# Layer 1 of a two-layer attention kernel: q loaded in the preceding slot, four coefficient instructions, GpSimd's last low part behind the next row's first combination

## Chip, core and metric

One core of one Trainium2 chip runs the whole program. The metric is the device time of one execution in microseconds. The median of the runs shown is compared, and one further execution was profiled.

## What is computed

Two layers, each added to its input. Layer 0 is a four-headed attention behind a convolution; the change does not touch it. Layer 1, for each of B = 2 images of C = 192 channels and N = 64 x 64 = 4096 positions, with xf the normalised image as [N, C]:

```python
xn = (xf - mu) * jax.lax.rsqrt(var + EPS) * ln_w + ln_b
Q, K, V = xn @ Wq.T, xn @ Wk.T, xn @ Wv.T
S = jnp.einsum('bnd,bmd->bnm', Q, K)
attn1 = jax.nn.softmax(S, axis=-1)
attn2 = jnp.square(jax.nn.relu(S))
e1, e2 = (jnp.exp(w1), jnp.exp(w2))
attn = e1 / (e1 + e2) * attn1 + e2 / (e1 + e2) * attn2
out = jnp.einsum('bnm,bmd->bnd', attn, V)      # then back to [b, c, h, w], + x
```

## The kernel before

Layer 1 takes an image after the other. A prologue makes, for the image, the scores' operand `kst` and the values `v_hl` in SBUF and the queries in `q_scratch` in HBM, all split into two float16 parts. Then the row loop runs over RB = 32 rows of 128 queries. A row's 4096 scores are worked in NQ = 4 pieces of 1024 columns. Each engine has its own hand-written sequence, cut into slots; in slot t VectorE and ScalarE finish row t and begin row t + 1, while TensorE makes the scores of row t + 1 and multiplies row t - 1's weights by v. Four slots stand alone, then a hardware loop holds two slots a pass (its branch lies between an odd slot and the next even one), and the last two stand alone. Semaphores alone tie the engines.

For piece c of a row, in order:

- TensorE, `score_half` (L1338): ten matmuls into PSUM `ps_s`, two groups of five. One group and one group of eight weighing matmuls (`weigh_group`, L1351) alternate, eight pairs a slot; `turn_output` (L1361) transposes the output of row t - 2 before the third weighing group.
- VectorE, `maximum` (L1578): `neg` = scaled, negated scores, with the piece's minimum as an accumulated output. `maximum` 3 is followed by L1583, L1585 (`m1`, one element per partition) and L1587 (`inv`), and frees PSUM for TensorE.
- ScalarE: `relu` and `square` (L1176, L1181) into `sqr[s]`, which is `vb` or `rn`; `exp_piece` (L1187) into `prob[s]`, which lies in `gp`, with the sums; `factors` (L1193) four factors of the row.
- VectorE, `coefficients` (L1593 to L1603): six small instructions, of [128, 1] or [128, 4], from sums and factors to `coef`.
- VectorE, `combine` (L1610), here called combination c: prob = prob x coef + sqr, 1024 columns, both tensors in SBUF.
- High part: `p_hi` = prob in float16; GpSimd casts pieces 0 and 1 (L1125), ScalarE pieces 2 and 3 (`high`, L1201). Low part: `p_lo` = prob - p_hi, all four on GpSimd (L1129), in the order high 0, low 0, high 1, low 1, low 2, low 3. Low 2 waits for combination 3 of its row.
- SyncE's queue: `turn_chunk` sends each part through a transposing DMA (L1066 high, L1068 low) into `at_hi`, `at_lo`, which TensorE weighs with v. Behind piece 0 stand `load_q` of row t + 2 (L1047), `store` of row t - 2 (L1058) and `load_res` (L1053).

VectorE's slot t: combination 3 of row t - 1; `copy_output` of row t - 2 (L1615, L1618: PSUM to `ob`, scaled by `back`); maximum 0 of row t + 1; coefficients of row t; combination 0; maximum 1; combination 1; `add_output` of row t - 2 (L1628, from PSUM and `res`); maximum 2; combination 2; maximum 3.

Of the kernel before, what the change touches and what calls it, by code (L numbers as in the profile page):

```python
# [817 lines left out]
def layer1(nc, x, o_dram, weights, consts, m_dram, r_dram, res_dram, q_dram, out):  # L818
# [6 lines left out]
    with ExitStack() as ctx:  # L825
# [16 lines left out]
        MX, CO = NQ + 3, 6  # L842
        KC = KT // NQ
        HIGH_ACT = (2, 3)
# [109 lines left out]
        relued = sem("relued")  # L954
        exped = sem("exped1")
        squared = sem("squared")
        c_op = sem("c_op")
        p_made = sem("p_made")
        t_full = sem("t_full")
        hi_made = [sem(f"hi_made{i}") for i in range(NQ)]  # L960
        lo_made = sem("lo_made1")
# [14 lines left out]
        with nc.Block() as block:  # L976
            @block.sync
            def _(sp):
# [8 lines left out]
                def image(b):  # L987
# [73 lines left out]
                    def turn_chunk(row, s, c, first=False):  # L1061
# [5 lines left out]
                        sp.wait_ge(lo_made, NQ * (RB * b + row) + c + 1)  # L1067
# [15 lines left out]
                    load_q(1, 1)  # L1083
                    slot(0, 0, True)
                    slot(1, 1, True)
                    for t in range(2, RB):
                        slot(t, t % 2, more_q=t < RB - 2)
# [9 lines left out]
            def _(pool):  # L1097
# [6 lines left out]
                for b in range(B):  # L1104
# [13 lines left out]
                    def split(row, s, first=False):  # L1118
                        for c in range(NQ):
                            cols = slice(c * QB, (c + 1) * QB)  # L1120
                            if c not in HIGH_ACT:
                                pool.wait_ge(p_made, NQ * (RB * b + row) + c + 1)
                                if not first:
                                    pool.wait_ge(turned[c], 32 * (RB * b + row))
                                pool.tensor_copy(p_hi[:, cols], prob[s][:, cols]).then_inc(hi_made[c], 1)  # L1125
                            pool.wait_ge(hi_made[c], RB * b + row + 1)
                            if c == 2:
                                pool.wait_ge(p_made, NQ * (RB * b + row) + NQ)
                            pool.tensor_tensor(p_lo[:, cols], prob[s][:, cols], p_hi[:, cols], ALU.subtract).then_inc(lo_made, 1)  # L1129

                    for row in range(RB):
                        split(row, row % 2, row == 0 and b == 0)

            @block.scalar
            def _(act):
# [3 lines left out]
                for b in range(B):  # L1139
# [31 lines left out]
                    def relu(row, s, c, first=False):  # L1171
                        cols = slice(c * QB, (c + 1) * QB)
                        act.wait_ge(mx_op, MX * (RB * b + row) + c + 1)
                        if not first:
                            act.wait_ge(p_made, NQ * (RB * b + row - 2) + c + 1)
                        act.activation(sqr[s][:, cols], neg[:, c, :], ACT.Relu, scale=top[:, 3:4]).then_inc(relued, 1)  # L1176

                    def square(row, s, c):
                        cols = slice(c * QB, (c + 1) * QB)
                        act.wait_ge(relued, NQ * (RB * b + row) + c + 1)  # L1180
                        act.activation(sqr[s][:, cols], sqr[s][:, cols], ACT.Square, scale=inv[:, s:s + 1]).then_inc(squared, 1)  # L1181

                    def exp_piece(row, s, c, first=False):
                        act.wait_ge(mx_op, MX * (RB * b + row) + c + 1)
                        if not first:
                            act.wait_ge(lo_made, NQ * (RB * b + row - 2) + c + 1)
                        act.activation(prob[s][:, c * QB:(c + 1) * QB], neg[:, c, :], ACT.Exp,  # L1187
                                       bias=nbias[:, s, c:c + 1], scale=-1.0,
                                       accum_out=sums[:, s, c:c + 1]).then_inc(exped, 1)

                    def factors(row, s):
# [559 lines left out]
```

## Time and profile before

| | us |
|---|---|
| median of 3 runs | 3659.16 (3658.95 to 3661.98) |
| the profiled execution's own time | 3657.04 |
| its span in the trace | 3655.3 |
| PE busy over the span | 3214.4 (88%) |
| DVE busy | 2191.9 (60%) |
| ACT busy | 2117.3 (58%) |
| POOL busy | 1023.0 (28%) |

The first image's row loop fills about 2257 to 2869 us, the second's about 3043 to 3653; the rest is layer 0 and the images' prologues. PE is TensorE, DVE VectorE, ACT ScalarE, POOL GpSimd, SPq the queue of SyncE. A row in order of time has its start in us from the span's start, its duration in us, engine, line, operation, output <- inputs, shape, and how many instructions in a row of the same kind were merged; in brackets stand the idle time of the engine before it and what ended it. An instruction of VectorE that stands in line behind another shows a start some 0.08 us ahead of the other's end. "issue" means that the engine waited for nothing that the profile shows. A row on stretches of time has the stretch, its length, then busy time (and number of instructions) of PE, PEld, DVE, ACT and POOL, the granted TensorE clock as a share of full speed, the share of the DMA engines and GB/s. A row on one line of code has the number of instructions and the shortest, median and longest duration in ns.

### The profile page before, as it was taken

How to read it: one execution, taken by the hardware profiler on the slowest of the kernel's cores; microseconds unless marked ns; L12 is line 12 of the kernel's file. 1: busy time of each engine (PE TensorE's matmuls, PEld its weight loads, DVE VectorE, ACT ScalarE, POOL GpSimd, SP SyncE). 2: the span in 40 equal slices, each digit the busy share in tenths (PEclk: the TensorE clock that was granted, in tenths of full speed). 3: DMA queues.
4: the chain of work that ended last, by engine and by line, in shares of the span. 5: the costliest groups of instructions: out<-in, count | busy, mean ns of one | idle time of the engine just before them, and what ended most of it. 6: DMA issues, size and time to landing. Idle time of an engine off the chain costs nothing. (4 is left out here: it accounts for less than half of the span.)

```text
span 3655.3 us, 48153 instructions
## 1 busy us (share of the span) xinstructions
PE 3214.4 (88%) x16424; PEld 1273.0 (35%) x16424; DVE 2191.9 (60%) x2585; ACT 2117.3 (58%) x2306; POOL 1023.0 (28%) x510
## 2 busy tenths in 40 slices
PE   1249999999999999999999768999999668999998
PEld 0012222222322223222222224555555334555554
DVE  4755254552446523475210255999999547999997
ACT  0016655556555565555666314888888126888886
POOL 0211002111021020110200032555555233555555
PEclk9669999999999999999999879999999789999999
DMA  6130213112121121220200223766666534766666
GB/s 183 44 75 19 59 40 70 43 33 59 41 62 42 41 58 42 45 56 24 57 10 7 67 77 94 133 131 132 130 130 130 120 100 101 133 130 133 129 130 124
DMA packets 691174, 295.70 MB, mean 81 GB/s; under 512 B 603314, under 2 KB 645042, under 8 KB 689266
## 3 DMA queue, kind: packets, MB, share of 16 engines
q1 hardware_dynamic: 690996, 293.45, 37.4%
q8 instruction: 96, 1.57, 0.2%
q14 instruction: 82, 0.67, 0.1%
HBM read 95.46 MB, written 34.28 MB: 35 GB/s over the span
## 5 line engine op out<-in xcount | busy, mean ns | idle before, releaser
L440 ACT ACTIVATE prob<-ps_s,cur 128x1024 f32<-128x1024 f32 x1024 | 1084.5, 1110 | 738.5 <-PE ps_s L514 737.0
L527 PE MATMUL ps_a<-prob,vt 128*64 128x512 f32 x4096 | 995.2, 607 | 0.0
L1338 PE MATMUL ps_s<-kst,qs 128*128 128x512 f16 x2560 | 638.5, 382 | 67.7 <-DMA qs<-q_scratch 65.3
L1129 POOL TENSOR_TENSOR p_lo<-gp,p_hi 128x1024 f16<-128x1024 f32 x256 | 547.4, 2139 | 321.2 <-DVE gp L1610 281.1
L1351 PE MATMUL ps_o<-v_hl,at_hi 128*128 128x384 f16 x2048 | 553.4, 331 | 22.6 <-DMA at_lo<-p_lo 19.7
L508 PE MATMUL ps_s<-q_a,k_a 128*128 128x512 f16 x2048 | 534.6, 383 | 7.3 <-issue 2.9
L1351 PE MATMUL ps_o<-v_hl,at_lo 128*128 128x192 f16 x2048 | 507.9, 249 | 0.0
L527 PEld LDWEIGHTS ps_a<-prob,vt 128*64 128x64 f32 x4096 | 249.1, 136 | 411.8 <-issue 410.2
L1338 PEld LDWEIGHTS ps_s<-kst,qs 128*128 128x128 f16 x2560 | 240.3, 98 | 306.8 <-issue 79.8
L1578 DVE TENSOR_SCALAR_CACHE_REDUCE neg<-ps_s,mix 128x1024 f32<-128x1024 f32 x256 | 326.1, 1274 | 23.6 <-PE ps_s L1338 23.4
L508 PEld LDWEIGHTS ps_s<-q_a,k_a 128*128 128x128 f16 x2048 | 137.9, 97 | 516.2 <-ACT prob L440 436.9
L411 POOL TENSOR_TENSOR sq<-qk 112x1024 f32<-112x1024 f32 x32 | 59.6, 1892 | 919.3 <-DVE qk L610 919.3
L610 DVE SCALAR_TENSOR_TENSOR qk<-pad,vec,qk 112x2048 f32<-112x2048 f32 x128 | 290.3, 2345 | 0.0
L1187 ACT ACTIVATE gp<-neg,nbias 128x1024 f32<-128x1024 f32 x256 | 290.2, 1133 | 0.0
L685 DVE RECIPROCAL rden<-rden 128x512 f32<-128x512 f32 x32 | 107.3, 3353 | 296.6 <-DMA rden<-den_scratch 296.6
L1351 PEld LDWEIGHTS ps_o<-v_hl,at_hi 128*128 128x128 f16 x2048 | 202.7, 99 | 203.6 <-DMA at_lo<-p_lo 45.4
L1610 DVE SCALAR_TENSOR_TENSOR gp<-gp,coef,rn 128x1024 f32<-128x1024 f32 x128 | 259.2, 2028 | 17.9 <-DVE neg L1578 7.9
L1610 DVE SCALAR_TENSOR_TENSOR gp<-gp,coef,vb 128x1024 f32<-128x1024 f32 x128 | 259.9, 2030 | 11.5 <-DVE neg L1578 4.7
L593 DVE TENSOR_SCALAR pad<-ps_h,vec 112x512 f32<-112x512 f32 x96 | 72.2, 752 | 291.5 <-PE ps_h L457 291.3
L457 PE MATMUL ps_h<-z,w 96*112 96x512 f32 x384 | 187.8, 624 | 38.8 <-DMA z<-z_scratch 38.8
L1351 PEld LDWEIGHTS ps_o<-v_hl,at_lo 128*128 128x128 f16 x2048 | 202.8, 99 | 44.3 <-issue 0.5
L1176 ACT ACTIVATE vb<-neg,top 128x1024 f32<-128x1024 f32 x128 | 146.0, 1141 | 116.5 <-DVE neg L1578 116.2
(176 smaller groups left out, 2865.1 us busy)
## 6 DMA issues: line engine op xcount, KB each, us to landing
z<-z_scratch SPq DMA_DIRECT2D x96, 384.0 KB, 3.8
sq<-rn_scratch SPq DMA_DIRECT2D x16, 768.0 KB, 10.4
qs<-q_scratch SPq DMA_DIRECT2D x64, 128.0 KB, 2.5
gn_x<-in_x SPq DMA_DIRECT2D x4, 1536.0 KB, 18.6
z_scratch<-gn_x SPq DMA_DIRECT2D x4, 1536.0 KB, 11.6
q_a<-hi SPq DMA_DIRECT2D x64, 96.0 KB, 2.3
rden<-den_scratch SPq DMA_DIRECT2D x64, 96.0 KB, 2.2
o_scratch<-o_s SPq DMA_DIRECT2D x64, 96.0 KB, 1.9
```

Of the source, the lines that this page charges most:

```text
L440: act.activation(prob[:, a % PR, :], ps_s[:, a % 2, :], ACT.Exp, bias=cur[:, slot:slot + 1], scale=1.0 / SPLIT).then_inc(exped, 1)
L457: ins = pe.matmul(ps_h[0:KR, bank, :], w[:, slot, t, 0:KR], z[:, c % ZS, t, :], start=(t == 0), stop=(t == CT - 1))
L508: pe.matmul(ps_s[:, n % 2, h * CH:(h + 1) * CH], k_a[:, slot, m * P:(m + 1) * P], q_a[:, slot, cols], start=True, stop=False)
L527: ins = pe.matmul(ps_a[h * HALF:(h + 1) * HALF, j % 2, :], vt[:, slot, m, :], prob[:, a % PR, h * CH:(h + 1) * CH], start=(m == 0), stop=( ...
L610: ins = dve.scalar_tensor_tensor(out=out, in0=src, scalar=vec[0:KR, slot, 1 + tap:2 + tap], in1=out, op0=ALU.mult, op1=ALU.add)
L1129: pool.tensor_tensor(p_lo[:, cols], prob[s][:, cols], p_hi[:, cols], ALU.subtract).then_inc(lo_made, 1)
L1176: act.activation(sqr[s][:, cols], neg[:, c, :], ACT.Relu, scale=top[:, 3:4]).then_inc(relued, 1)
L1187: act.activation(prob[s][:, c * QB:(c + 1) * QB], neg[:, c, :], ACT.Exp, bias=nbias[:, s, c:c + 1], scale=-1.0, accum_out=sums[:, s, c:c + ...
L1338: ins = pe.matmul(ps_s[:, c % 2, h * CH:(h + 1) * CH], qs[:, s, qt, :], kst[:, ktile, cols], start=(t == 0), stop=(t == len(terms) - 1))
L1351: ins = pe.matmul(ps_o[:, s * CH:s * CH + wide], a[:, s, kt, :], v_hl[:, kt, 0:wide], start=(kt == 0 and t == 0), stop=(kt == KT - 1 and t ...
L1578: dve.tensor_scalar(neg[:, c, :], ps_s[:, c % 2, :], mix[:, 6:7], None, ALU.mult, ALU.min, accum_out=nbias[:, s, c:c + 1]).then_inc(mx_op, 1)
L1610: dve.scalar_tensor_tensor(out=prob[s][:, cols], in0=prob[s][:, cols], scalar=coef[:, s, c:c + 1], in1=sqr[s][:, cols], op0=ALU.mult, op1= ...
```

## The change

- `load_q(t + 3)` stands in slot t before the transpositions of piece 3, into the buffer that row t + 1 leaves; rows 0 to 2 are loaded ahead. Before, `load_q(t + 2)` stood behind those of piece 0.
- `coefficients` has four instructions: `back` first, with `mix[:, 5:6]` in the place of a constant; then product, scaling by `back` and sum in one, with an accumulated output; reciprocal; `coef`. It gets a wait for `ob_made`, an earlier instruction of VectorE itself. `relu` no longer carries the scale, which moves into L1585's counterpart (L1615), now a constant factor and a minimum against `top[:, 3:4]`; `top[:, 3:4]` is made once, with one more small instruction.
- GpSimd's low 2 no longer waits for combination 3; low 3 waits for combination 0 of the next row.
- VectorE's `add_output` stands behind combination 2, before maximum 3.
- ScalarE's slot begins with square 0, which was third; it waits for `inv`.
- Semaphores per piece (`p_made[c]`, `exped[c]` and others) take the place of shared counters, and rows outside the image are skipped in the functions (`live`) instead of by flags. The order of the first and last slots is as it was but for the moves above.

```diff
@@ sync
                         for c in range(NQ):
+                            if c == NQ - 1 and more_q:
+                                load_q(t + 3, 1 - s)
                             turn_chunk(t, s, c, first and t < 2 and b == 0)
                             if c == 0:
-                                if more_q:
-                                    load_q(t + 2, s)
                                 if not first:
                                     store(t - 2, s)
@@ gpsimd
+                    def low(row, s, c):
+                        if not 0 <= row < RB:
+                            return
+                        cols = slice(c * QB, (c + 1) * QB)
+                        pool.wait_ge(hi_made[c], RB * b + row + 1)
+                        if c == 3 and row < RB - 1:
+                            pool.wait_ge(p_made[0], RB * b + row + 2)
+                        pool.tensor_tensor(p_lo[:, cols], prob[s][:, cols], p_hi[:, cols], ALU.subtract).then_inc(lo_made[c], 1)
+
+                    def slot(t, s):
+                        high(t, s, 0)
+                        low(t, s, 0)
+                        high(t, s, 1)
+                        low(t, s, 1)
+                        low(t, s, 2)
+                        low(t, s, 3)
@@ scalar
-                        exp_piece(t, s, NQ - 1, older)
+                        square(t, s, 0)
+                        exp_piece(t, s, 3)
                         factors(t, s)
-                        square(t, s, 0)
@@ vector
-                            dve.tensor_scalar(m1[:, s:s + 1], nbmin[:, s:s + 1], mix[:, 7:8], -1.0, ALU.mult, ALU.min).then_inc(mx_op, 1)
+                            dve.tensor_scalar(m1[:, s:s + 1], nbmin[:, s:s + 1], 1.0 / GAIN, top[:, 3:4], ALU.mult, ALU.min).then_inc(mx_op, 1)
                     def coefficients(row, s):
...
-                        dve.tensor_tensor(part[:, :], fac[:, s, :], sums[:, s, :], ALU.mult).then_inc(c_op, 1)
+                        if not isinstance(row, int) or row > 1:
+                            dve.wait_ge(ob_made, RB * b + row - 1)
+                        dve.scalar_tensor_tensor(out=back[:, s:s + 1], in0=m1[:, s:s + 1], scalar=mix[:, 5:6],
+                                                 in1=m1[:, s:s + 1], op0=ALU.mult, op1=ALU.mult).then_inc(c_op, 1)
                         dve.wait_ge(c_op, at + 1)
-                        dve.tensor_reduce(total[:, :], part[:, :], AX_X, ALU.add).then_inc(c_op, 1)
-                        dve.scalar_tensor_tensor(out=back[:, s:s + 1], in0=m1[:, s:s + 1], scalar=1.0 / (GAIN * GAIN),
-                                                 in1=m1[:, s:s + 1], op0=ALU.mult, op1=ALU.mult).then_inc(c_op, 1)
+                        dve.scalar_tensor_tensor(out=part[:, :], in0=fac[:, s, :], scalar=back[:, s:s + 1], in1=sums[:, s, :],
+                                                 op0=ALU.mult, op1=ALU.mult, accum_out=total[:, :]).then_inc(c_op, 1)
+                        dve.wait_ge(c_op, at + 2)
+                        dve.reciprocal(total[:, :], total[:, :]).then_inc(c_op, 1)
                         dve.wait_ge(c_op, at + 3)
-                        dve.tensor_tensor(total[:, :], total[:, :], back[:, s:s + 1], ALU.mult).then_inc(c_op, 1)
+                        dve.tensor_scalar(coef[:, s, :], fac[:, s, :], total[:, 0:1], mix[:, 4:5], ALU.mult, ALU.mult).then_inc(c_op, 1)
...
+                        maximum(t + 1, 1 - s, 2)
                         combine(t, s, 2)
-                        if new:
-                            maximum(t + 1, 1 - s, 3)
+                        add_output(t - 2, s, j)
+                        maximum(t + 1, 1 - s, 3)
```

GpSimd, one slot late in an image, before (with the semaphores each instruction waits for; `hi_made3` stands at low 3):

```order
384 L1125 CAST p_hi<-gp 128x1024 [waits turned0,p_made]
385 L1129 TENSOR_TENSOR p_lo<-gp,p_hi 128x1024 [waits hi_made0]
386 L1125 CAST p_hi<-gp 128x1024 [waits turned1,p_made]
387 L1129 TENSOR_TENSOR p_lo<-gp,p_hi 128x1024 [waits hi_made1]
388 L1129 TENSOR_TENSOR p_lo<-gp,p_hi 128x1024 [waits p_made,hi_made2]
389 L1129 TENSOR_TENSOR p_lo<-gp,p_hi 128x1024 [waits hi_made3]
```

The same place after the change (`p_made1_0` is combination 0):

```order
384 L1125 CAST p_hi<-gp 128x1024 [waits turned0,p_made1_0]
385 L1134 TENSOR_TENSOR p_lo<-gp,p_hi 128x1024 [waits hi_made0]
386 L1125 CAST p_hi<-gp 128x1024 [waits turned1,p_made1_1]
387 L1134 TENSOR_TENSOR p_lo<-gp,p_hi 128x1024 [waits hi_made1]
388 L1134 TENSOR_TENSOR p_lo<-gp,p_hi 128x1024 [waits hi_made2]
389 L1134 TENSOR_TENSOR p_lo<-gp,p_hi 128x1024 [waits p_made1_0,hi_made3]
```

The instructions stand in the same order; the wait for a combination moved from low 2 to low 3, and there it is the next row's.

VectorE in the loop, from combination 1 to maximum 3's end, before:

```order
1049 L1610 SCALAR_TENSOR_TENSOR gp<-gp,coef,rn 128x1024 [waits mx_op,squared]
1050 L1628 SCALAR_TENSOR_TENSOR ot<-ps_t,unscale,res 96x128 [waits ot_out1,res_in1,t_full]
1051 L1628 SCALAR_TENSOR_TENSOR ot<-ps_t,unscale,res 96x128
1052 L1575 REGISTER_ALU
1053 L1577 REGISTER_ALU [waits s_full]
1054 L1578 TENSOR_SCALAR neg,nbias<-ps_s,mix 128x1024 [waits exped1]
1055 L1580 REGISTER_ALU
1056 L1610 SCALAR_TENSOR_TENSOR gp<-gp,coef,rn 128x1024 [waits mx_op,squared]
```

After the change:

```order
1011 L1644 SCALAR_TENSOR_TENSOR gp<-gp,coef,rn 128x1024 [waits mx_op,squared1_1]
1012 L1605 REGISTER_ALU
1013 L1608 TENSOR_SCALAR neg,nbias<-ps_s,mix 128x1024 [waits exped1_2,s_full]
1014 L1610 REGISTER_ALU
1015 L1644 SCALAR_TENSOR_TENSOR gp<-gp,coef,rn 128x1024 [waits mx_op,squared1_2]
1016 L1666 SCALAR_TENSOR_TENSOR ot<-ps_t,unscale,res 96x128 [waits ot_out1,res_in1,t_full]
1017 L1666 SCALAR_TENSOR_TENSOR ot<-ps_t,unscale,res 96x128
```

The two instructions of `add_output` moved from before maximum 2 to behind combination 2.

## Rows read from the trace of the kernel before

**Rows 1.** Busy time by stretch, the first image's row loop.
```profile
2301.00:2836.00 535.00, 496.64 (x3061) 279.55 (x3059) 505.26 (x719) 435.53 (x547) 307.11 (x174) 1.00 0.68 131
```

**Rows 2.** Order of time, DVE, one slot of the loop, combination 0 to coefficients.
```profile
2453.40 0.29 DVE L1603 TENSOR_SCALAR coef<-fac,total,mix 128x4 f32<-128x4 f32 x1
2453.73 1.28 DVE L1610 SCALAR_TENSOR_TENSOR gp<-gp,coef,vb 128x1024 f32<-128x1024 f32 x1
...
2456.37 3.04 DVE L1610 SCALAR_TENSOR_TENSOR gp<-gp,coef,vb 128x1024 f32<-128x1024 f32 x1 [0.15 <-DVE neg L1578]
2459.33 0.59 DVE L1628 SCALAR_TENSOR_TENSOR ot<-ps_t,unscale,res 96x128 f32<-96x128 f32 x2
2459.85 1.27 DVE L1578 TENSOR_SCALAR_CACHE_REDUCE neg<-ps_s,mix 128x1024 f32<-128x1024 f32 x1
...
2461.27 2.52 DVE L1610 SCALAR_TENSOR_TENSOR gp<-gp,coef,vb 128x1024 f32<-128x1024 f32 x1
...
2465.34 0.22 DVE L1585 TENSOR_SCALAR m<-nbmin,mix 128x1 f32<-128x1 f32 x1
...
2465.67 1.27 DVE L1610 SCALAR_TENSOR_TENSOR gp<-gp,coef,vb 128x1024 f32<-128x1024 f32 x1
...
2469.06 0.18 DVE L1593 TENSOR_TENSOR part<-fac,sums 128x4 f32<-128x4 f32 x1
...
2469.93 2.16 DVE L1603 TENSOR_SCALAR coef<-fac,total,mix 128x4 f32<-128x4 f32 x1
2472.12 1.28 DVE L1610 SCALAR_TENSOR_TENSOR gp<-gp,coef,rn 128x1024 f32<-128x1024 f32 x1
```

**Rows 3.** Order of time, POOL, in the same slot.
```profile
2455.08 1.04 POOL L1125 CAST p_hi<-gp 128x1024 f16<-128x1024 f32 x1 [1.93 <-DVE gp L1610]
2456.20 2.13 POOL L1129 TENSOR_TENSOR p_lo<-gp,p_hi 128x1024 f16<-128x1024 f32 x1
...
2469.93 2.13 POOL L1129 TENSOR_TENSOR p_lo<-gp,p_hi 128x1024 f16<-128x1024 f32 x1 [0.70 <-ACT p_hi L1201]
```

**Rows 4.** Order of time, DVE, the slot before it, which follows the loop's branch.
```profile
2447.30 1.29 DVE L1610 SCALAR_TENSOR_TENSOR gp<-gp,coef,rn 128x1024 f32<-128x1024 f32 x1 [0.38 <-issue]
...
2451.18 1.99 DVE L1599 TENSOR_TENSOR total<-total,back 128x1 f32<-128x1 f32 x1
```

**Rows 5.** Order of time, PE, score groups 0, 1 and 3 of a slot.
```profile
2462.36 1.25 PE L1338 MATMUL ps_s<-kst,qs 128*128 128x512 f16 x5 [0.88 <-DMA qs<-q_scratch]
...
2464.43 1.24 PE L1338 MATMUL ps_s<-kst,qs 128*128 128x512 f16 x5
...
2469.07 1.24 PE L1338 MATMUL ps_s<-kst,qs 128*128 128x512 f16 x5
```

**Rows 6.** Order of time, DVE, the first image's first combination 0 and its last row.
```profile
2269.17 1.28 DVE L1610 SCALAR_TENSOR_TENSOR gp<-gp,coef,vb 128x1024 f32<-128x1024 f32 x1
...
2843.86 2.48 DVE L1610 SCALAR_TENSOR_TENSOR gp<-gp,coef,rn 128x1024 f32<-128x1024 f32 x2
...
2846.78 4.61 DVE L1610 SCALAR_TENSOR_TENSOR gp<-gp,coef,rn 128x1024 f32<-128x1024 f32 x2
```

**Rows 7.** Order of time, POOL, in that last row.
```profile
2845.21 2.03 POOL L1125 CAST p_hi<-gp 128x1024 f16<-128x1024 f32 x1 [1.41 <-DVE gp L1610]
2847.32 2.98 POOL L1129 TENSOR_TENSOR p_lo<-gp,p_hi 128x1024 f16<-128x1024 f32 x1
```

**Rows 8.** Line L1068, the transpositions of low parts: from issue to landing.
```profile
DMA to landing us min/median/max: 3.0/3.2/4.8
```

**Rows 9.** Lines L673 and L630: copies of one and of two elements per partition.
```profile
L673 DVE COPY cur<-tabs x8: 146/150/155, 72.3 to 1649.3; 128x1 f32 x6, 128x1 f32<-128x1 f32 x2
L630 DVE COPY cura<-alpha x8: 169/170/170, 171.8 to 1761.7; 128x2 f32 x6, 128x2 f32<-128x2 f32 x2
```

**Rows 10.** Order of time, DVE and POOL, at the program's start.
```profile
69.37 2.25 DVE L694 TENSOR_SCALAR tabs<-temp 128x8 f32<-128x8 f32 x1 [20.11 <-DMA temp<-in_temperature]
...
70.65 0.95 POOL L402 MEMSET vt<- 128x1024 f32 x1
```

More of the change, by code:

```diff
@@ L1083, in image @@
                     load_q(1, 1)
+                    load_q(2, 0)
                     slot(0, 0, True)
@@ L1131, in _, with high @@
-                    for row in range(RB):
-                        split(row, row % 2, row == 0 and b == 0)
+                    def high(row, s, c):
+                        if not 0 <= row < RB:
+                            return
+                        cols = slice(c * QB, (c + 1) * QB)
+                        pool.wait_ge(p_made[c], RB * b + row + 1)
+                        if b or row:
+                            pool.wait_ge(turned[c], 32 * (RB * b + row))
+                        pool.tensor_copy(p_hi[:, cols], prob[s][:, cols]).then_inc(hi_made[c], 1)
@@ L1134, in _ @@
+                    def slot(t, s):
[5 more added lines that the diff above has]
+                        low(t, s, 3)
+                    for t in range(RB + 1):
+                        slot(t, t % 2)
             @block.scalar
@@ L1184, in exp_piece @@
+                        act.wait_ge(relued[c], RB * b + row + 1)
+                        act.activation(sqr[s][:, cols], sqr[s][:, cols], ACT.Square, scale=inv[:, s:s + 1]).then_inc(squared[c], 1)
+                    def exp_piece(row, s, c):
+                        if not live(row):
+                            return
                         act.wait_ge(mx_op, MX * (RB * b + row) + c + 1)
-                        if not first:
-                            act.wait_ge(lo_made, NQ * (RB * b + row - 2) + c + 1)
+                        if past(row, 2):
+                            act.wait_ge(lo_made[c], RB * b + row - 1)
@@ L1194, in factors, with high @@
                                        bias=nbmin[:, s:s + 1], scale=-1.0).then_inc(fac_made, 1)
-                    def high(row, s, c, first=False):
+                    def high(row, s, c):
+                        if not live(row):
+                            return
                         cols = slice(c * QB, (c + 1) * QB)
-                        act.wait_ge(p_made, NQ * (RB * b + row) + c + 1)
-                        if not first:
+                        act.wait_ge(p_made[c], RB * b + row + 1)
+                        if past(row, 1):
@@ L1221, in slot @@
+                        exp_piece(t + 1, 1 - s, 2)
                         square(t, s, 3)
-                        high(t, s, 2, older and t == 0)
-                        if new:
-                            relu(t + 1, 1 - s, 3, first)
-                    fresh = b == 0
-                    for c in range(NQ):
-                        relu(0, 0, c, fresh)
-                        if c < NQ - 1:
-                            exp_piece(0, 0, c, fresh)
-                    slot(0, 0, True, fresh, fresh)
@@ L1232, in _ @@
-                    slot(1, 1, True, False, fresh, fresh)
+                        high(t, s, 2)
+                        relu(t + 1, 1 - s, 3)
+                    slot(-1, 1)
+                    slot(0, 0)
+                    slot(1, 1)
                     with act.Fori(0, RB // 2 - 2) as r:
@@ L1236, in _ @@
                     slot(RB - 2, 0)
-                    slot(RB - 1, 1, False)
-                    high(RB - 1, 1, 3)
+                    slot(RB - 1, 1)
+                    slot(RB, 0)
             @block.tensor
@@ L1621, in add_output @@
                     def add_output(row, s, j):
+                        if not live(row):
+                            return
                         dve.wait_ge(t_full, RB * b + row + 1)
@@ L1662, in _ @@
                         slot(2 * r + 5, 1, r + 1)
-                    slot(RB - 2, 0, RB // 2 - 2)
-                    slot(RB - 1, 1, RB // 2 - 2, False)
-                    combine(RB - 1, 1, 3)
-                    for row in (RB - 2, RB - 1):
-                        copy_output(row, row % 2)
-                        add_output(row, row % 2, RB // 2 - 1)
+                    for t in range(RB - 2, RB + 2):
+                        slot(t, t % 2, t // 2 - 1)
 TILE_BLOCKS = [(0, 4), (8, 9), (1, 5), (2, 6), (10, 11), (3, 7)]
```

128 lines of the change are left out of this document (58 added, 70 removed).

## The prediction

> **What bounds the kernel now.** I read the stretch view first, then VectorE and GpSimd side by side in order of time through one slot, then TensorE, then the places where the two differ from the rule. In the row loop of layer 1 TensorE is busy 496.64 of 535 us at a granted clock of 1.00, VectorE 505.26 [rows 1]; neither alone explains the period. One period is read from one "combination 0" (`combine(t, t, 0)`) to the next: 2453.73 to 2472.12, 18.39 us [rows 2], and 18.39 + 0.46 = 18.85 where the loop's branch lies in between (0.38 idle before combination 3 against none) [rows 4]. From the first combination 0 of an image to its last are 31 periods in 2843.86 - 2269.17 = 574.7 us [rows 6], 18.54 each.
>
> In that period VectorE never waits for TensorE. It waits for GpSimd. Combination 1 starts at 2456.37 and takes 3.04; GpSimd's subtraction began at 2456.20, ends at 2458.33, and the combination ends 1.08 later. Combination 2 likewise: 2.52 instead of 1.28. The last coefficient instruction (L1603, four numbers per partition) takes 2.16 instead of 0.29: it ends with the subtraction that began at 2469.93 and took 2.13 [rows 2, 3]. With the branch it is L1599 that takes 1.99 [rows 4]. So an instruction of VectorE with two SBUF inputs, or L1603's kind, and one of GpSimd exclude each other for the whole instruction. Stalls per slot: 1.76 + 1.24 + 1.87 = 4.9 us. Who asks first wins, and who waits gets the turn next: in the image's last slot a cast takes 2.03 instead of 1.04 because a combination runs until 2846.34 (2843.86 + 2.48; the cast ends 0.90 after that); combination 2, asked at 2846.78, waits for the cast's end at 2847.24; the subtraction asked at 2847.32 waits for the combination and ends 2.0 after it, at 2850.30 [rows 6, 7].
>
> TensorE's slot without a wait: eight groups, 2.07 apart (2462.36 to 2464.43), with the output's transposition 4.64 for two (2464.43 to 2469.07), so 6 x 2.07 + 4.64 = 17.06, about 17.0 us [rows 5]. Its waits (0.88 for q in that row) cost nothing now, since VectorE comes later anyway. 17.0 is the floor of any change to the other engines.
>
> **The change, part by part.** Time 0 is the start of combination 0; prices from [rows 2, 3, 4, 6, 7].
>
> *The held-back low part.* GpSimd now does low 3 of the old row, high 0, low 0, high 1, low 1, low 2. Low 3 is asked at 1.35 (2455.08 - 2453.73), ends 3.48. Combination 1 asks at 2.64, runs to 4.56. High 0 asked at 3.56, ends 4.56 + 0.90 = 5.46; low 0 asked 0.08 later at 5.54, ends 7.67. VectorE's next instruction starts at 4.48, the maximum; 1.42 later, at 5.90, combination 2 asks, and ends at 7.67 + 1.08 = 8.75. High 1 ends 9.65, low 1 runs 9.73 to 11.86, low 2 asks at 11.94. Before, combination 1 ended at 5.68 and combination 2 at 10.06, so 1.1 and 1.3 us are won.
>
> *`add_output` moved behind combination 2.* Its 0.52 (2459.33 to 2459.85) sat in a wait and sat there free; now it stands after one: 8.67 to 9.19. That 0.52 is paid, and is in the figures that follow. The output's store on SyncE waits for it at about 9.3, with the transposition of high 1 behind, which is made only at 9.65: nothing.
>
> *Maximum 3 and the three small instructions.* The maximum starts at 9.19. In [rows 2] it starts 0.08 ahead of combination 2's end, at 2463.71, L1585 follows 1.63 and combination 3 1.96 later. So L1585 comes at 10.81, and combination 3 asks at 11.14, or 11.60 with the branch. Both are before 11.94. Combination 3 then takes the turn at 11.86 and ends at 12.94, low 2 at 14.93. **This is the choice that decides the forecast**: 10.81 lies inside low 1, where in the rows of before L1585 always found GpSimd idle. Between the ends: it does not wait at all (0.22 as now), or it waits to 11.89 as L1603 does. I take the first, by the nearest row on that side: two-element copies take 169 to 170 ns and one-element copies 146 to 155 [rows 9], so a one-element instruction looks like another mode than those of even size, and L1585 writes one element. It is not strong.
>
> *Four coefficient instructions instead of six.* Combination 3 to the first of them is 3.39 (2465.67 to 2469.06), so they start 2.21 after VectorE is free at 12.86: 15.07. GpSimd's low 2 ended at 14.93 and low 3 is held back, so nothing meets them. Unhindered, six take 0.87 + 0.33 = 1.20 [rows 2]. Of four, three cost 0.20, 0.20 and 0.33 as now; the one that now also writes a sum may add an accumulator read, bounded by 0 and 0.23 more (after the maximum, which has one, the next instruction starts 0.15 behind its end, 2461.27 against 2461.12; without one it starts 0.08 ahead of it). I take 1.12 for all four. By itself the edit is worth 0.1 us; what it buys is mostly the held-back part's: 1.87 of stall gone. Combination 0 comes at 16.19, with or without the branch, which falls into combination 3's wait.
>
> *ScalarE* does the same work; its chain from maximum 2 to the factors stays under 15.1 us, and the first square now first waits for L1587, which is early. No price, bound 0 to 0.3.
>
> *q loaded a slot earlier.* The 0.88 goes: else TensorE would need 17.9. On SyncE the load stands behind the transposition of low 2 and ahead of high 3, its wait (scores of the next row) over since about 9. No one waits for it.
>
> *TensorE against 16.2.* Low 3 is made at 3.48, its transposition lands 3.2 later [rows 8], 6.75 with the issue. TensorE's last two groups of the slot need it; from there the scores for maximum 3 are ready 2.3 later, at 9.05, against 9.19: just in time. From there on TensorE falls 0.8 behind per slot, as 17.0 - 16.2. After one slot maximum 3 is at 9.8 to 9.9, combination 3 asks at 11.8 (no branch) or 12.3 (branch). In the latter case low 2 asks first, ends at 14.07, combination 3 at 15.15, and the coefficients and combination 0 follow 2.2 later, at 18.4; TensorE has caught up by then. So a fast and a slow slot alternate, (16.2 + 18.4) / 2 = **17.3**.
>
> *The ends of an image.* The first period has no old low 3, and low 2 comes before combination 3: 16.9. Behind the last combination 0 GpSimd has one subtraction more, 2.13 + 0.08 = 2.2.
>
> *Sum.* 16.9 + 30 x 17.3 = 535.9 against 574.7, less 38.8; plus 2.2: 36.6 an image, 73 for both. The profiled execution took 3657.0 (span 3655.3), so 3584; the median of the three runs lies 2.1 above it: **3586**. Its own range: from the floor, 16.9 + 30 x 17.0, which gives 3568, to 17.5 in place of 17.3, 3598.
>
> **Rivals.**
>
> *L1585 waits.* Then it ends at 11.89, combination 3 asks at 12.01, 0.07 behind low 2. Low 2 runs to 14.07, combination 3 to 15.15, combination 0 at 18.4, each slot, branch or not. Periods 17.2, 17.6 (no output yet), 29 x 18.4 = 568.4, less 6.3, plus 2.2: 4.1 an image, 8 in all, **3651**. It decides as soon as combination 3 asks after 11.94. For it: L1603 is of the same kind and waits every time. Against: the copies above. A landing of 4.8, the longest now [rows 8], at every row would end there too: scores at 10.65, combination 3 after 12.6.
>
> The Trainium skill (SBUF — State Buffer, "Who interferes with whom") says that a `tensor_scalar` in a two-port mode takes the pair of ports that GpSimd uses and that the loser blocks for the whole instruction. L1603 agrees, with 2.16 us. The Trainium skill (VectorE: DVE Perf Modes, "What auto-detection actually checks") gives that mode to a single source in SBUF whose outermost non-unit dimension and the destination's are both even or equal; one element to one element is equal, so by its letter L1585 waits and the time is this rival's, 3651, against 3586 by the copies. No row of before shows a one-element `tensor_scalar` beside a subtraction.
>
> *The turn is not handed over.* If GpSimd's next instruction, 0.08 behind its last, went ahead of a waiting combination, low 3, high 0 and low 0 would run through to 6.81 before combination 1; combination 2 would end at 12.4, combination 3 at 16.7, combination 0 come at 19.9. That is 1.4 over now, 30 times, plus 2: 43 an image, **3745**, slower. Before, no third instruction stood behind the subtraction, so a lost turn cost nothing. For it: L694 waited 2.25 us, from 69.37 to 71.62, through a row of GpSimd fills whose last ended at 71.60 [rows 10]. Against: the three hand-overs of [rows 6, 7], with the same 0.08 between the instructions; the fills had no waits between them. It decides as soon as GpSimd runs three instructions without one of VectorE's.
>
> *TensorE alone is the bound*, nothing slips past 11.94: 17.0, **3568**.
>
> **Chances.** The forecast 0.53; L1585 waits (or late landings) 0.34; TensorE alone 0.08; no hand-over 0.05. The range goes from 3566 to 3656: it holds all but the last. About 0.2% (7 us) is what a measurement of this kernel tells from no change; 3651 lies on that line, so half of its 0.34 is faster, 0.15 the same, 0.02 slower. Faster 0.53 + 0.08 + 0.17 = 0.78, same 0.15, slower 0.07.
>
> **What the changed kernel's profile would show.** Right: combination 1 at about 1.9 us, combination 2 at 2.9, combination 3 at 1.3 to 1.8 or 3.1 in turn; all four coefficient instructions unhindered; L1585 at 0.22 inside low 1; no wait of TensorE for q; GpSimd idle between low 2 and combination 0; the periods in two sizes with a mean of 17.0 to 17.5. The first rival shows L1585 at about 1.1 and combination 3 at 3.1 in each slot, at 18.4. The second shows low 3, high 0 and low 0 with 0.08 between them and combination 1 over 4 us. What would make me wrong besides: an accumulator read that costs more than 0.3, or a transposition of low 3 that lands after 7.2, so that TensorE's scores and not the ports set combination 3.

## The result and the profile after

| | before | after |
|---|---|---|
| median, us | 3660.07 (4 runs, 3658.95 to 3661.98) | **3574.49** (4 runs, 3574.14 to 3575.17) |
| profiled execution / span, us | 3657.04 / 3655.3 | 3574.26 / 3572.5 |

The ratio is 0.9767, with an interval of 0.9753 to 0.9781: 2.3% faster. The forecast was 3586 with a range of 3566 to 3656.

Busy time by stretch, after the change, 475 us of the first and of the second image's row loop (columns as in [rows 1]):

```profile
2301.00:2776.00 475.00, 466.25 (x2924) 269.59 (x2922) 425.86 (x663) 413.76 (x525) 357.16 (x166) 1.00 0.74 141
3047.00:3522.00 475.00, 470.94 (x2973) 275.66 (x2972) 409.37 (x673) 418.24 (x534) 371.03 (x170) 1.00 0.75 143
```

TensorE's share rose from 496.64 / 535 = 93% [rows 1] to 98% and 99%, at the same granted clock of 1.00; VectorE's fell from 94% to 90% and 86%. GpSimd's rose from 57% to 75% and 78% with no more work: its casts now stand in line behind combinations.

One slot in order of time, VectorE, from the last combination of the slot before (the counterpart of [rows 2]):

```profile
2402.77 3.22 DVE L1644 SCALAR_TENSOR_TENSOR gp<-gp,coef,rn 128x1024 f32<-128x1024 f32 x1 [0.38 <-issue]
...
2408.20 0.22 DVE L1627 SCALAR_TENSOR_TENSOR back<-m,mix 128x1 f32<-128x1 f32 x1 [0.23 <-DVE neg L1608]
2408.45 0.22 DVE L1630 SCALAR_TENSOR_TENSOR part<-fac,back,sums 128x4 f32<-128x4 f32 x1
2408.60 0.08 DVE L1630 DVE_READ_ACCUMULATOR part<-fac,back,sums 128x1 f32 x1
2408.72 0.16 DVE L1633 RECIPROCAL total<-total 128x1 f32<-128x1 f32 x1
2408.92 0.29 DVE L1635 TENSOR_SCALAR coef<-fac,total,mix 128x4 f32<-128x4 f32 x1
2409.24 1.28 DVE L1644 SCALAR_TENSOR_TENSOR gp<-gp,coef,vb 128x1024 f32<-128x1024 f32 x1
...
2411.89 2.00 DVE L1644 SCALAR_TENSOR_TENSOR gp<-gp,coef,vb 128x1024 f32<-128x1024 f32 x1 [0.15 <-DVE neg L1608]
...
2415.24 2.83 DVE L1644 SCALAR_TENSOR_TENSOR gp<-gp,coef,vb 128x1024 f32<-128x1024 f32 x1 [0.15 <-DVE neg L1608]
2418.00 0.59 DVE L1666 SCALAR_TENSOR_TENSOR ot<-ps_t,unscale,res 96x128 f32<-96x128 f32 x2
...
2420.14 0.21 DVE L1615 TENSOR_SCALAR m<-nbmin,top 128x1 f32<-128x1 f32 x1
2420.39 0.16 DVE L1617 RECIPROCAL inv<-m 128x1 f32<-128x1 f32 x1
2420.47 1.80 DVE L1644 SCALAR_TENSOR_TENSOR gp<-gp,coef,vb 128x1024 f32<-128x1024 f32 x1
```

GpSimd in the same stretch (the counterpart of [rows 3]):

```profile
2400.68 4.23 POOL L1134 TENSOR_TENSOR p_lo<-gp,p_hi 128x1024 f16<-128x1024 f32 x2
2410.67 2.13 POOL L1134 TENSOR_TENSOR p_lo<-gp,p_hi 128x1024 f16<-128x1024 f32 x1 [5.76 <-DVE gp L1644]
2412.76 2.03 POOL L1125 CAST p_hi<-gp 128x1024 f16<-128x1024 f32 x1
2414.86 2.13 POOL L1134 TENSOR_TENSOR p_lo<-gp,p_hi 128x1024 f16<-128x1024 f32 x1
2416.94 2.03 POOL L1125 CAST p_hi<-gp 128x1024 f16<-128x1024 f32 x1
2419.05 5.21 POOL L1134 TENSOR_TENSOR p_lo<-gp,p_hi 128x1024 f16<-128x1024 f32 x2
```

The handing over is there as forecast. Low 3 begins at 2410.67 and ends at 2412.80; combination 1, which asked in it, ends 1.09 later; the cast, which asked in that, takes 2.03 instead of 1.04. Combinations 1 and 2 take 2.00 and 2.83 (3.04 and 2.52 before), and the four coefficient instructions stand free of GpSimd: L1635 takes 0.29 where L1603 took 2.16.

The last rows show the fast ending of a slot: combination 3 asks at 2420.47, before low 1 ends at 2421.18, and takes 1.80. The first rows show the slow one: there, behind the loop's branch, it asks at 2402.77 only. Low 1 (the first of the two subtractions merged from 2400.68) ends at 2400.68 + 2.13 = 2402.81, low 2 goes next and ends at 2400.68 + 4.23 = 2404.91, and combination 3 ends 1.08 after that, at 2405.99. So a combination whose row starts 0.05 us ahead of low 1's end (2402.767 against 2402.818, unrounded) still loses the turn. In this trace five combinations 3 that started up to 0.07 ahead lost it, and all that started 0.10 or more ahead got it; in q_and_hold some lost it at up to 0.09.

Lines L1615, L1125 and the transpositions of L1067 over the whole program:

```profile
L1615 DVE TENSOR_SCALAR m<-nbmin,top x64: 212/214/217, 2267.2 to 3539.0; 128x1 f32<-128x1 f32 x64
L1125 POOL CAST p_hi<-gp x128: 1028/2034/2049, 2272.7 to 3553.4; 128x1024 f16<-128x1024 f32 x128
DMA to landing us min/median/max: 3.0/3.1/5.1
```

From combination 0 to combination 0 the first image now has 16.28 and 18.37 us in turn (12 slots of about 18.37 in all) and the second mostly 16.28, 16.28, 16.67, 18.38 (8 slow ones). Why the one slips at every second slot and the other at every fourth no run shows. The 31 periods add up to 532.28 and 525.03 us, against 574.69 and 574.61 before.

### The profile page after: what moved, and what is told of

It is laid out like the page before. It is cut to its first block and busy times, and to the rows that moved or that the text cites. A ratio compares the mean times of both kernels' runs of the same rounds, so it can differ in the third digit from the quotient of the medians.

```text
span 3572.5 us, 48126 instructions
## 1 busy us (share of the span) xinstructions
PE 3193.4 (89%) x16424; PEld 1278.0 (36%) x16424; DVE 2039.8 (57%) x2522; ACT 2107.3 (59%) x2306; POOL 1172.5 (33%) x510
## 5 line engine op out<-in xcount | busy, mean ns | idle before, releaser
L1134 POOL TENSOR_TENSOR p_lo<-gp,p_hi 128x1024 f16<-128x1024 f32 x256 | 588.0, 2308 | 252.6 <-DVE gp L1644 237.7
L1361 PEld LDWEIGHTS ps_s<-kst,qs 128*128 128x128 f16 x2560 | 244.3, 98 | 246.4 <-issue 26.4
L1125 POOL CAST p_hi<-gp 128x1024 f16<-128x1024 f32 x128 | 252.5, 1973 | 76.6 <-DVE gp L1644 76.6
L1644 DVE SCALAR_TENSOR_TENSOR gp<-gp,coef,rn 128x1024 f32<-128x1024 f32 x128 | 240.6, 1882 | 17.3 <-issue 7.1
L1644 DVE SCALAR_TENSOR_TENSOR gp<-gp,coef,vb 128x1024 f32<-128x1024 f32 x128 | 239.1, 1868 | 10.7 <-DVE neg L1608 7.0
L416 POOL TENSOR_TENSOR lo<-u,hi 112x1024 f16<-112x1024 f32 x32 | 100.9, 3153 | 370.4 <-DVE hi L659 370.4
## 6 DMA issues: line engine op xcount, KB each, us to landing
gn_x<-in_x SPq DMA_DIRECT2D x4, 1536.0 KB, 18.7
```

Source lines behind the costliest of these rows:

```text
L1361: ins = pe.matmul(ps_s[:, c % 2, h * CH:(h + 1) * CH], qs[:, s, qt, :], kst[:, ktile, cols], start=(t == 0), stop=(t == len(terms) - 1))
L1644: dve.scalar_tensor_tensor(out=prob[s][:, cols], in0=prob[s][:, cols], scalar=coef[:, s, c:c + 1], in1=sqr[s][:, cols], op0=ALU.mult, op1= ...
```

## The experiments

Every run stands beside runs of the kernel before on the same chip (3658.5 to 3660.0). Periods are read from combination 0 to combination 0 in the order of time; a mean period leaves out an image's first. Unless said otherwise a diff is against the changed kernel.

**m1_two: does L1615 stand free because it writes one element?** The same line with two elements per partition; the second is filled and read by no one.

```diff
-dve.tensor_scalar(m1[:, s:s + 1], nbmin[:, s:s + 1], 1.0 / GAIN, top[:, 3:4], ALU.mult, ALU.min).then_inc(mx_op, 1)
+dve.tensor_scalar(m1[:, 2 * s:2 * s + 2], nbmin[:, 2 * s:2 * s + 2], 1.0 / GAIN, top[:, 3:4], ALU.mult, ALU.min).then_inc(mx_op, 1)
... (m1 and nbmin are widened to four elements, and their other uses take element 2 * s)
```

> The changed kernel, but L1615 (minimum against top) works on two elements per partition instead of one, the second a filler that nobody reads. Theory of the prediction: VectorE's one-source instructions of even size wait for a running GpSimd instruction, a one-element one does not. Then L1615 waits until low 1 ends (about 1.0 us instead of 0.21), combination 3 asks behind low 2 in every slot, every period is 18.4 us, and the time is about 3650 us. Rival: the size does not matter, L1615 never takes the shared path (then 0.22 us, periods 16.3 and 18.4 as in the changed kernel, 3574 us).

Measured: 3653.73, ratio 0.9986 (0.9977 to 0.9995). Its line, and VectorE and GpSimd in one slot:

```profile
L1616 DVE TENSOR_SCALAR m<-nbmin,top x64: 228/1070/1789, 2267.5 to 3614.5; 128x2 f32<-128x2 f32 x64
```

```profile
2410.06 1.07 DVE L1616 TENSOR_SCALAR m<-nbmin,top 128x2 f32<-128x2 f32 x1
2411.16 0.16 DVE L1618 RECIPROCAL inv<-m 128x1 f32<-128x1 f32 x1
2411.70 2.57 DVE L1645 SCALAR_TENSOR_TENSOR gp<-gp,coef,rn 128x1024 f32<-128x1024 f32 x1 [0.38 <-issue]
```

```profile
2408.97 4.22 POOL L1135 TENSOR_TENSOR p_lo<-gp,p_hi 128x1024 f16<-128x1024 f32 x2
```

The instruction ends at 2411.13, where low 1 ends, combination 3 asks behind low 2, and every slot but an image's first and last is 18.4 long (mean 18.33). The line waits so in 62 of its 64 executions; the other two are each image's first, with GpSimd idle. This is the first rival, forecast at 3651, brought about by one element more. It settles the choice that the forecast rested on: of this instruction the one-element form does not take part in the exclusion, the two-element form does. Alignment is no rival here, since `s` takes both elements of `m1` in turn and neither waits.

**no_hold, q_late: the two edits undone one at a time.** no_hold puts the wait of low 2 back and lets low 3 run; q_late puts the load of q back behind the transpositions of piece 0.

```diff
# no_hold
-                        if c == 3 and row < RB - 1:
-                            pool.wait_ge(p_made[0], RB * b + row + 2)
+                        if c == 2:
+                            pool.wait_ge(p_made[3], RB * b + row + 1)
```

> The changed kernel, but GpSimd's low parts wait as before: low 2 for combination 3 of its row, low 3 for its high part alone. Theory (the held-back low part is what brings the gain): low 2 and low 3 fall on the coefficients again, add_output has lost its cover, combination 0 comes 18.9 us after the last one, about 3680 us, slower than the kernel before by 0.5%. Rival (the four coefficient instructions bring it): near 3580 us.

> The changed kernel, but q is loaded where it was before, two rows ahead behind piece 0's transpositions. Theory: TensorE is the bound of the changed kernel at 16.9 us a slot; its wait for q comes back (0.9 us a slot before), the slot is 17.5 to 17.8 us, and the time 3605 to 3630 us. Rival: the ports of VectorE and GpSimd still set the slot (17.2 us in image 1) and hide the load, then 3575 to 3580 us.

Measured: no_hold 3677.89 (1.0053, 1.0038 to 1.0068), slower than before; q_late 3629.99 (0.9917, 0.9901 to 0.9932). In no_hold the stall has moved to the first coefficient instruction, as VectorE's order of time shows:

```profile
2416.43 2.18 DVE L1627 SCALAR_TENSOR_TENSOR back<-m,mix 128x1 f32<-128x1 f32 x1 [0.22 <-DVE neg L1608]
```

and combinations 1 and 2 both take 3.03 (2.52 for the second before), since `add_output` no longer lies between them: the rest of the change without the hold-back costs 0.5%. L1627 has one element too, but two inputs of SBUF, and in 24 of its 64 executions it waits. It starts 0.08 ahead of low 2's end here (2414.38 + 2.13 = 2416.51) and low 3 goes first, as at combination 3 above. In q_late the slots are 17.64 and 18.36, and TensorE waits 16 times for q in 300 us, 18.7 us in all (0.73 in the slot from 2404). That is the upper edge of what was expected.

**q_only, hold_only, q_and_hold: the two edits put alone, and together, into the kernel before.**

```diff
# against before; hold_only is the second part, q_only the first
+                            if c == NQ - 1 and more_q:
+                                load_q(t + 3, 1 - s)
                             turn_chunk(t, s, c, first and t < 2 and b == 0)
...
-                                if more_q:
-                                    load_q(t + 2, s)
... (rows 0 to 2 loaded ahead)
-                            if c == 2:
-                                pool.wait_ge(p_made, NQ * (RB * b + row) + NQ)
+                            if c == 3 and row < RB - 1:
+                                pool.wait_ge(p_made, NQ * (RB * b + row + 1) + 1)
```

> The kernel before with one part of the change, q loaded in the preceding slot. Theory: VectorE's stalls behind GpSimd set the slot there (18.55 us), TensorE's wait for q lies beside them, so nothing moves: 3655 to 3663 us, with TensorE waiting elsewhere for as long. Rival: the wait for q (0.9 us a slot) is on the path: about 3605 us.

> The kernel before with one part of the change, low 2 free of combination 3 and low 3 held back to the next row's combination 0; six coefficient instructions, q late, add_output where it was. Theory: VectorE's own period falls to 16.4 us, and TensorE with its wait for q becomes the bound, as in the changed kernel with the late q (17.6 and 18.4 in turn): 3620 to 3635 us. Rival: without the four coefficient instructions little is won: 3645 to 3660 us.

> The kernel before with two parts of the change, the early q and the held-back low part; six coefficient instructions, add_output before maximum 2, ScalarE's order as before. Theory: these two are the whole gain. q_only gave nothing (3660), hold_only 26 us (3633), together they free VectorE and TensorE: 3566 to 3576 us. Rival: the other edits carry part of it: 3585 us or more.

| | time | ratio | mean period, first image |
|---|---|---|---|
| before | 3659 | 1 | 18.55 |
| q_only | 3659.95 | 1.000 (0.999 to 1.0009) | 18.55 |
| hold_only | 3632.93 | 0.9929 (0.9914 to 0.9944) | 18.08 |
| q_and_hold | 3581.33 | 0.9793 (0.9779 to 0.9806) | 17.22 |

What TensorE waited for in 300 us of the loop (2301 to 2601), first in q_only, then in hold_only:

```profile
PE ps_t L1362 <- DVE ob L1619: 21.8, 16, 1.7
```

```profile
PE ps_s L1338 <- DMA qs<-q_scratch: 21.3, 16, 2.3
```

Alone, the early q is worth nothing: where TensorE is not the bound its wait only moves, from q to `ob`. Alone, the hold-back gives 26 us: VectorE could do a slot of 16.3, as q_and_hold shows, but TensorE waits 1.3 for q in nearly every slot, and slots of 17.8 and 18.4 alternate. Together they give 78 us, three times the sum. q_and_hold is slower than the 3566 to 3576 expected of it and faster than its rival's 3585. The remaining edits (four coefficients, `add_output`, ScalarE's order, semaphores) are worth 9.6 us in the medians, 3581.33 (3575.67 to 3586.3) against 3571.74 (3566.41 to 3574.7) on the same chip. The profiled spans, 3573.9 and 3572.9, stand 1 apart only, but their periods show more: they add up to 1064.2 us over both images in q_and_hold and to 1057.2 in changed_again, with 22 and 20 slow slots. Two stretches outside the row loops hide these 7 us: in q_and_hold the first score came 3.8 earlier in this one execution, and the two first combinations 0 came 1.6 sooner after their images' first scores. Which of the remaining edits brings the 7 stays open: two of them, undone one at a time below, change nothing that can be measured.

**low2_waits: the slip taken away.** Low 2 also waits for combination 3, so that it can't go ahead of it.

```diff
+                        if c == 2:
+                            pool.wait_ge(p_made[3], RB * b + row + 1)
                         if c == 3 and row < RB - 1:
                             pool.wait_ge(p_made[0], RB * b + row + 2)
```

> The changed kernel, and low 2 waits for combination 3 of its row, so that it never takes the turn ahead of it. Theory: the 18.4 us slots are those in which low 2 asks first; with these gone both images run at TensorE's 16.9 us. Image 1 had 17.2, image 2 had 16.9, so 0.25 x 30 = 7 us less: 3567 us. Rival: low 2 now ends later and falls on the first coefficient instructions, 0.1 to 1 us a slot: 3574 to 3600 us.

Measured: **3551.56**, 0.9706 (0.9693 to 0.9719), 23 us under the changed kernel and 15 under the 3567 expected, which took TensorE's floor at 16.9. No slot of 18.4 is left; the mean period is 16.69 in both images. By stretch, and then TensorE around the output's transposition:

```profile
2301.00:2776.00 475.00, 474.24 (x3013) 281.48 (x3012) 384.30 (x682) 422.35 (x540) 354.32 (x171) 1.00 0.77 145
```

```profile
2417.74 1.24 PE L1363 MATMUL ps_s<-kst,qs 128*128 128x512 f16 x5
2418.82 0.38 PE L1386 MATMUL ps_t<-ident,ob 128*96 128x128 f32 x2
...
2420.02 1.24 PE L1363 MATMUL ps_s<-kst,qs 128*128 128x512 f16 x5
```

TensorE is busy 474.24 of 475 us: this is the floor, and it is lower than the 17.0 of the forecast. From the group ahead of the transposition to the next it is 2.28 here, and was 2.58 in the kernel before, 2466.49 to 2469.07 [rows 5]:

```profile
2466.49 1.24 PE L1338 MATMUL ps_s<-kst,qs 128*128 128x512 f16 x5
2467.86 0.40 PE L1361 MATMUL ps_t<-ident,ob 128*96 128x128 f32 x2
```

```profile
2467.30 0.42 DVE L1618 SCALAR_TENSOR_TENSOR ob<-ps_o,back,ob_lo 128x192 f32<-128x192 f32 x1
```

The transposition begins 1.37 behind the scores' start there and 1.08 here: before, TensorE waited 0.3 for `ob`, which L1618 finished at 2467.72, without a mark in the row. 7 x 2.06 + 2.28 = 16.7. VectorE now waits for TensorE, 59.3 us in 475 against 18.4 in the changed kernel, in the two kernels' lists of waits (changed kernel first):

```profile
DVE neg L1608 <- PE ps_s L1361: 18.4, 31, 1.3
```

```profile
DVE neg L1610 <- PE ps_s L1363: 59.3, 87, 1.4
```

**six_coef, six_again, add_out_back, changed_again: the small edits.** six_coef and six_again are the changed kernel with six coefficient instructions, in which `back` keeps its new scalar from SBUF and the new wait for `ob_made` stays; in add_out_back `add_output` stands before maximum 2 again; changed_again is the changed kernel itself, beside six_again, add_out_back and q_and_hold on one chip.

```diff
# six_coef, six_again
+dve.tensor_tensor(part[:, :], fac[:, s, :], sums[:, s, :], ALU.mult).then_inc(c_op, 1)
+dve.wait_ge(c_op, at + 1)
+dve.tensor_reduce(total[:, :], part[:, :], AX_X, ALU.add).then_inc(c_op, 1)
 dve.scalar_tensor_tensor(out=back[:, s:s + 1], in0=m1[:, s:s + 1], scalar=mix[:, 5:6],
                          in1=m1[:, s:s + 1], op0=ALU.mult, op1=ALU.mult).then_inc(c_op, 1)
...
-dve.scalar_tensor_tensor(out=part[:, :], in0=fac[:, s, :], scalar=back[:, s:s + 1], in1=sums[:, s, :],
-                         op0=ALU.mult, op1=ALU.mult, accum_out=total[:, :]).then_inc(c_op, 1)
...
+dve.tensor_tensor(total[:, :], total[:, :], back[:, s:s + 1], ALU.mult).then_inc(c_op, 1)
```

> The changed kernel with the six coefficient instructions of before in the place of the four. Theory: with no GpSimd instruction beside them, six cost 0.1 us more than four, and TensorE hides most of that: 3574 to 3580 us. Rival: the four are worth a stall each slot: 3600 us or more.

> The changed kernel with add_output before maximum 2 again. The prediction took its 0.52 us a slot as paid. Theory now: combination 3 waits for low 1 until 11.86 anyway, so the 0.52 falls into that wait or into VectorE's wait for TensorE's scores, and the place does not matter: 3570 to 3577 us. Rival: it is paid, 0.5 x 60: about 3545 us; or moving it back pushes maximum 2 and slots lose more: 3585 us.

> The changed kernel itself beside the other two on one chip. Both theories: 3574 us, with 16.3 and 18.4 us slots mixed; six_coef at 3569 us was on another chip, so a number near 3569 here would say that the two are the same, one near 3575 that six instructions are the faster.

> six_coef once more, beside the changed kernel on one chip. Theory: a VectorE that is 0.2 us a slot slower gains less on TensorE and loses the turn to low 2 once in four slots instead of once in two (image 1), so it is 4 to 6 us faster than the changed kernel. Rival: the difference was the chip's: within 2 us of changed_again.

Measured: six_coef 3569.04 (0.9757, 0.9743 to 0.977), which looked 5 us faster than the change and gave rise to six_again. On one chip six_again has 3571.84 and changed_again 3571.74: the same. A fast slot of six_coef is 16.47 long, 0.19 more than 16.28, but a longer slot slips more seldom (every fourth, mean 17.03), and the two cancel. The six of the kernel before cost less: in q_and_hold, where they too stand free of GpSimd, a fast slot is 16.32. add_out_back has 3574.09 (0.9767): the same too, with the same slots of 16.28 and 18.37.

**last_row_act: the last row's chain cut.** low2_waits, with ScalarE casting high 0 and high 1 in an image's last row, where GpSimd works alone at the end.

```diff
# against low2_waits
+                        if isinstance(t, int) and t == RB - 1:
+                            high(t, s, 0)
+                            high(t, s, 1)
                         high(t, s, 2)
... (GpSimd leaves these two out in the last row)
```

> The kernel low2_waits (3552 us), and in an image's last row ScalarE makes high parts 0 and 1 as well, after its last square. Theory: the change made the stretch behind the last combination 0 of an image 2.8 to 3.2 us longer, all of it GpSimd's queue of seven instructions; two casts less, which each take 2.0 us there, give 2 to 4 us an image: 3544 to 3548 us. Rival: the lows still follow the combinations and only fill the gaps: 3550 to 3552 us.

Measured: 3549.35 (0.9702, 0.9689 to 0.9716). The tails from the last combination 0 to the last output are 26.23 and 24.21, against 27.33 and 26.19 in low2_waits: 3.1 us less in the traces. The median lies between the two theories' ranges, 3544 to 3548 and 3550 to 3552. The medians of the two kernels differ by 2.2 and the intervals overlap, so the times alone don't tell it from low2_waits. Both beat the changed kernel and the one before.

## Why the prediction was right, and by how much it was not

The mechanism, the pattern of slots and the sign came out; two terms of the sum were mis-sized in opposite directions. In the spans: 91.99 us won in the periods (77.6 forecast), 5.96 lost in the tails (4.4), 3.25 ahead of the combinations 0 (nothing taken, bound 0.3 for ScalarE). 91.99 - 5.96 - 3.25 = 82.78, the difference of the spans, against 73. So the forecast came within 11.5 us of the time partly because the errors have opposite signs.

- **VectorE's slot** was forecast at 16.19, and is 16.28: low 3 is asked 0.08 later than worked out, the coefficients start another 0.08 later behind combination 3, and they take 0.08 less. Combinations 1 and 2 were to take 1.9 and 2.9 and take 2.00 and 2.83. All of low 3, the casts and low 0 stand within 0.1 us of the places worked out.
- **L1615 does not wait**: 212 to 217 ns in 64 of 64, and 62 of these start inside a subtraction. The choice was right, though the prediction called it not strong, and m1_two shows that the element count decides it, as the prediction had guessed from copies. The Trainium skill (VectorE: DVE Perf Modes, "What auto-detection actually checks"), read by its letter, spoke for the rival; the trace does not agree for one element, and agrees for two. The first rival was the right price for the wrong branch: 3651 forecast, 3653.73 measured where L1615 was made to wait.
- **The turn is handed over**: the second rival, 3745, falls. A combination that asked in a cast or a subtraction at least 0.10 us ahead of its end came next and ended some 1.08 us after it, and a cast that asked in a combination ended 0.9 after that, with 0.08 between GpSimd's instructions. The prediction put the last moment at low 2's asking, 0.08 behind low 1's end; it lies about 0.09 ahead of that end. The Trainium skill (SBUF — State Buffer, "Who interferes with whom"), by which the loser blocks for the whole instruction, agrees with these rows.
- **TensorE's floor, 17.0, is the step that failed.** It is 16.69. The 4.64 taken for two groups with the transposition [rows 5] held 0.3 of waiting for `ob`, which the kernel before hid. A distance of starts was taken for work. With 16.69 TensorE falls behind by 0.4 a fast slot and not by 0.8, so a slip should come less often: 20 slow slots were counted and not 30. That the one causes the other is argued; six_coef points the same way, where a fast slot of 16.47 leaves 0.2 to fall behind and 14 slow slots were counted. So the mean is 17.18 and 16.94 in the place of 17.3, which is 14.4 us of the 92.0. The third rival, TensorE alone at 17.0 and 3568, came out at 16.69 and 3551.56 in low2_waits, under the forecast's lower end.
- **The slip** needed no late landing. Combination 3 asks 0.71 us ahead of low 1's end without the branch (2420.47 to 2421.18), so some 0.33 with it, of which 0.09 is of no use; TensorE's lag of 0.4 eats the rest in one slot.
- **`add_output`'s 0.52** was said to be paid. It is not: add_out_back gives the same slots. From combination 0 to combination 3 GpSimd's chain sets the time, and combination 3 takes its turn at low 1's end whether it asks 0.7 or 1.2 us ahead.
- **Four coefficients** were given 0.1 us a slot. From the first to combination 0 it is 1.04 in the trace (2408.20 to 2409.24) against 1.17 for the old six standing free in q_and_hold, but they begin 2.21 behind combination 3's end and not 2.13, so a fast slot gains 0.04. The wait for `ob_made` is the one thing new there; it wasn't tested alone. six_again costs 0.19 a fast slot and the same time, so a gain here is worth nothing: it goes in more slips.
- **ScalarE's order** had a bound of 0.3 once, and costs 0.6 and 1.1 us ahead of the two images' first combination 0. Square 0 now stands before the last exponential and the factors, and there VectorE waits for them, while in a later slot it doesn't. q_and_hold, in which ScalarE's order is the old one, has 16.38 us from the first score to combination 0, against 17.23 in changed_again. Of the first image, the four kernels with the old order have 15.98 to 16.55, the ten with the new one 16.80 to 17.52; the order alone was not put back in any run. ScalarE, then VectorE, ahead of the first combination 0 after the change:

```profile
2267.81 1.13 ACT L1207 ACTIVATE vb<-vb,inv 128x1024 f32<-128x1024 f32 x1
2268.85 1.13 ACT L1215 ACTIVATE gp<-neg,nbias 128x1024 f32<-128x1024 f32 x1
...
2269.98 0.28 ACT L1223 ACTIVATE fac<-nbias,nbmin 128x4 f32<-128x4 f32 x1
```

```profile
2270.30 0.22 DVE L1627 SCALAR_TENSOR_TENSOR back<-m,mix 128x1 f32<-128x1 f32 x1 [1.32 <-ACT fac L1223]
```

- **The first image's first score** comes at 2254.20 instead of 2252.62, which is the other 1.6 of the 3.3. In the runs of the study it comes anywhere from 2250.9 (q_and_hold) to 2256.4 (hold_only), so it is scatter of the part ahead and no work of the change.
- **The tails** were forecast at +2.2 and are +3.17 and +2.79. GpSimd's last subtraction ends 2.1 later after the last combination 0, as worked out. The rest comes behind it: TensorE starts on the last pieces 1.54 after that end (0.72 before), since it waits for the transposition of an earlier low part. With the low part held back the first image's tail lies anywhere from 26.78 (add_out_back) to 28.37 (q_late), 28.22 here, so a part of its 3.17 need not be the hold-back's; the second's lies at 26.2 to 26.4. GpSimd and TensorE at this place, first after, then before:

```profile
2814.19 6.28 POOL L1134 TENSOR_TENSOR p_lo<-gp,p_hi 128x1024 f16<-128x1024 f32 x3
```

```profile
2822.01 0.34 PE L1374 MATMUL ps_o<-v_hl,at_hi 128*128 128x384 f16 x1 [2.02 <-DMA at_lo<-p_lo]
```

```profile
2852.36 6.28 POOL L1129 TENSOR_TENSOR p_lo<-gp,p_hi 128x1024 f16<-128x1024 f32 x3
```

```profile
2859.36 0.50 PE L1351 MATMUL ps_o<-v_hl,at_hi 128*128 128x384 f16 x1 [1.37 <-DMA at_lo<-p_lo]
```

## What to carry to other kernels

Where two engines exclude each other and the turn goes to whoever asks first, a slot's length is not a sum but depends on the order of asking: an instruction that comes 0.3 us late pays a whole one of the other engine, 2.1 us here. Here moving work to where the other engine is free brought more than shortening it, and a wait that fixes the order (low2_waits) may be worth more than it costs. A floor must be read from groups that have waited for nothing, since a wait that costs nothing today is counted as work by whoever adds up starts; and an edit that is worth nothing alone (q_only) may be worth 50 us behind another.

## What was not expected of the hardware

- One element per partition against two decides whether a scale-and-minimum of VectorE, from SBUF to SBUF, stands in line behind a subtraction of GpSimd: 0.214 us, waiting in none of 64, against a median of 1.07 us, and 80 us of the program.
- A one-element instruction with two tensor inputs of SBUF does wait (L1627 in no_hold, 2.18 us; L1599 before, 1.99 [rows 4], each in 24 of 64), while a reciprocal (L1617 at 2420.39) took its 0.16 inside a subtraction.
- Casts and subtractions of GpSimd hand the turn over in the gap of 0.08 us between them, with one limit: a combination that starts less than about 0.09 us ahead of the running instruction's end comes too late, and GpSimd's next goes first (2402.77 in the rows above).
